# A step table for each group of heads, and norm stages cut into single tiles

## The reference, cut to what matters

```python
x = L0_attn_x
x = x + layernorm(attn(layernorm(x)))        # k, q = latent part + rope part; softmax(q k / sqrt(32)) v; W_O
x = x + layernorm(ffn(layernorm(x)))

def attn(x):
    c_kv, c_q = x @ W_DKV + b_DKV, x @ W_DQ + b_DQ               # latent 128
    k_c, v_c, q_c = c_kv @ W_UK + b_UK, c_kv @ W_UV + b_UV, c_q @ W_UQ + b_UQ
    k_r, q_r = (x @ W_KR + b_KR) * pe, (x @ W_QR + b_QR) * pe    # one rope part for all heads
    ...
    return ctx @ W_O + b_O

def ffn(x):
    # routed: per token the 2 best experts, relu(x @ w_up)^2 @ w_down, weighted
    # shared: relu(x @ shared_up)^2 @ shared_down, with 1024 inner columns
    return routed + shared
```

## Time and profile before

| | |
|---|---|
| Runs | 1718.91, 1721.18, 1721.28 us, median 1721.18 |
| The profiled execution's own time | 1716.51 us |
| Its span (first to last instruction) | 1714.7 us |
| Granted TensorE clock, mean over the span | 0.965 of full |
| Instructions | 22207 |
| DMA | 270.57 MB, mean 158 GB/s |

### The profile page before, as it was taken

How to read it: one execution, slowest core, us unless ns; L and a number is a source line. 1 busy time by engine, 2 the same in 40 slices (tenths; PEclk the granted TensorE clock), 3 DMA queues, 4 the chain that set the end, 5 groups by cost and what they waited for, 6 DMA issues and landing times.

```text
span 1714.7 us, 22207 instructions
## 1 busy us (share of the span) xinstructions
PE 1594.9 (93%) x7386; PEld 1077.0 (63%) x7386; DVE 926.6 (54%) x1896; ACT 836.7 (49%) x1496; POOL 796.5 (46%) x820
## 2 busy tenths in 40 slices
PE   4798999999999899899999789998999999989997
PEld 3454655656556465565654568887666666657886
DVE  3666667575766666766653436445111111128998
ACT  2355456565565565645645434430333333346554
POOL 1167586676766776758669220002222222123341
PEclk9799999999999999999999889997999999989999
DMA  4647367465474663745761252123833433367773
GB/s 120 199 123 200 99 173 225 120 183 156 138 224 124 186 200 99 213 125 166 212 195 73 85 183 87 43 99 96 309 130 128 132 127 129 117 235 255 239 235 129
DMA packets 123767, 270.57 MB, mean 158 GB/s; under 512 B 15396, under 2 KB 27044, under 8 KB 117508
## 3 DMA queue, kind: packets, MB, share of 16 engines
q1 hardware_dynamic: 97256, 205.97, 39.9%
q0 software_dynamic: 12912, 41.82, 7.7%
q10 hardware_dynamic: 13488, 21.37, 3.4%
HBM read 154.03 MB, written 92.01 MB: 143 GB/s over the span
## 4 chain that ended last, share of the span: by engine, by line
PE 67%; DMA 9%; DVE 7%; POOL 7%; issue 5%; SPq 3%; ACT 2%; POOLq 0%; DVEq 0%; ACTq 0%
PE bank L109 10%; PE bank L677 10%; PE bank L733 8%; PE bank L756 8%; PE bank L655 8%; PE bank L592 4%; DMA a<-in_L_attn_x 4%; PE bank L576 4%; PE bank L562 4%; PE bank L581 3%; POOL a L1549 3%; PE bank L716 2%; SPq L1711 2%; DMA a<-kq_scratch 2%; DMA kq_scratch<-a 1%
## 5 line engine op out<-in xcount | busy, mean ns | idle before, releaser
L1549 POOL TENSOR_TENSOR a<-a 128x512 f32<-128x512 f32 x384 | 493.5, 1313 | 83.5 <-ACT a L1352 82.3
L1352 ACT ACTIVATE a<-bank 128x512 f32<-128x512 f32 x512 | 297.4, 597 | 204.0 <-PE bank L581 193.7
L866 DVE TENSOR_REDUCE a<-bank 128x1 f32<-128x512 f32 x512 | 324.0, 680 | 122.3 <-PE bank L562 121.6
L109 PE MATMUL bank<-a 128*128 128x512 f32 (+1 forms) x864 | 238.9, 401 | 8.7 <-DVE a L812 4.0
L576 PE MATMUL bank<-a 128*128 128x512 f32 x512 | 224.7, 439 | 12.3 <-ACT a L1352 12.2
L562 PE MATMUL bank<-a 128*128 128x512 f32 x512 | 188.2, 426 | 29.5 <-DVE a L866 15.1
L581 PE MATMUL bank<-a 68*128 68x512 f32 x512 | 208.2, 407 | 0.2 <-ACT a L1342 0.2
L655 PE MATMUL bank<-c 128*128 128x512 f32 x768 | 186.8, 403 | 21.4 <-ACT c L1404 12.0
L109 PEld LDWEIGHTS bank<-a 128*128 128x128 f32 (+1 forms) x864 | 159.7, 188 | 53.0 <-DVE a L875 4.5
L1621 POOL DMA_INDIRECT f<-h_scratch,f x79 | 75.0, 950 | 251.8 <-PE bank L716 229.1
L655 PEld LDWEIGHTS bank<-c 128*128 128x128 f32 x768 | 148.4, 194 | 59.1 <-issue 12.5
(11 more groups left out here) (186 smaller groups left out, 1896.0 us busy)
## 6 DMA issues: line engine op xcount, KB each, us to landing
a<-kq_scratch SPq DMA_DIRECT2D x192, 256.0 KB, 5.8
kq_scratch<-a SPq DMA_DIRECT2D x32, 1024.0 KB, 4.1
a<-a SPq DMA_DIRECT2D x80, 256.0 KB, 5.3
yp_scratch<-f ACTq DMA_DIRECT2D x79, 256.0 KB, 2.0
a<-in_L_attn_x SPq DMA_DIRECT2D x15, 1024.0 KB, 9.2
x_scratch<-a SPq DMA_DIRECT2D x8, 1024.0 KB, 4.8
h_scratch<-a SPq DMA_DIRECT2D x8, 1024.0 KB, 12.8
hT_scratch<-s SPq DMA_DIRECT2D x8, 1024.0 KB, 8.9
```

What stands on the lines that cost most here:

```text
L109: t = e.matmul(out, a[n], b[n], start=n == 0 and m == 0, stop=n == len(ah) - 1 and m == 2)
L866: e.tensor_reduce(K.mx[:, i, j:j + 1], K.MX[n % 3][:], AX.X, ALU.max).then_inc(Z.max, 1)
L1352: e.activation(K.pt[:, n % NP, :], K.SC[n % 2][:], ACT.Exp, scale=SCALE).then_inc(Z.exp, 1)
L1549: e.tensor_tensor(K.acc[:, j, :], a, K.pt[:, n % NP, :], ALU.add).then_inc(Z.acc, 1)
```

## The change: what it does

`STEP` gets a row of entries for each group (the digit in the name), and the entries count half steps: 2s stands between the scores of step s and its tops, 2s+1 behind the tops; an entry above 31 falls into the next unit. `beside_order` now returns all stages of a unit with their keys, and `attention_order` sorts them. `norm_order` has a stage for each tile: four "stat", one "aggr", "root", four "scale", and for "y" four "residual". The instructions, their sizes and their semaphores are the same. Since `after_order` uses `norm_order`, the list `rest` beside the shared FFN grows from 20 entries to 34.

```diff
@@ -118,7 +118,8 @@
 
 
 def norm_order(kind, b):
-    return [("stat", kind, b, 0), ("stat", kind, b, 1), ("root", kind, b), ("scale", kind, b, 0), ("scale", kind, b, 1)]
+    return ([("stat", kind, b, i) for i in range(4)] + [("aggr", kind, b), ("root", kind, b)]
+            + [("scale", kind, b, i) for i in range(4)] + [("residual", b, i) for i in range(4) if kind == "y"])
 
 
 def half_order(u):
@@ -138,46 +139,79 @@
     return ([("turn", b, k) for k in range(4)], [("proj", b, w) for w in ("kv", "q", "r")], [("v", b, i) for i in range(4)])
 
 
-STEP = {"last values": 2, "total": 2, "invert": 1, "k": 0, "q": 4, "divide": 3, "round": 5, "low": 6, "qr": 0,
-        "turn": (6, 7, 9, 12), "proj": (6, 14), "r": 4, "v": (4, 6, 10, 12), "project": (9, 10, 13, 15), "turn2": (2, 3, 8, 8),
-        "route": 12, "fold": 15, "rows": 14, "n": (0, 1, 3, 6, 9), "y": (0, 3, 4, 6, 7), "h": (0, 0, 2, 4, 7),
-        "values": (7, 11, 14), "tops": (3, 3, 4, 5, 5, 6, 8, 10, 12, 13, 14, 14, 16, 16, 16, 16)}
-
-
-def norm_at(kind, b):
-    return list(zip(STEP[kind], norm_order(kind, b)))
+STEP = {"last values0": 9, "total0": 8, "invert0": 10, "divide0": 2, "round0": 14, "low0": 15, "k0": 1, "q0": 3, "rows0": 27,
+        "values0": (15, 15, 29), "tops0": (3, 4, 5, 6, 6, 7, 10, 11, 14, 14, 16, 16, 16, 16, 16, 16), "last values1": 7,
+        "total1": 7, "invert1": 7, "divide1": 8, "round1": 24, "low1": 18, "k1": 9, "q1": 11, "rows1": 30,
+        "values1": (16, 23, 30), "tops1": (3, 3, 5, 5, 7, 8, 10, 10, 13, 14, 15, 15, 16, 16, 16, 16), "last values2": 7,
+        "total2": 6, "invert2": 8, "divide2": 5, "round2": 17, "low2": 21, "k2": 4, "q2": 5, "rows2": 30,
+        "values2": (12, 21, 31), "tops2": (3, 3, 6, 6, 6, 7, 8, 10, 12, 13, 13, 13, 16, 16, 16, 16), "last values3": 6,
+        "total3": 7, "invert3": 5, "divide3": 12, "round3": 23, "low3": 30, "k3": 0, "q3": 2, "rows3": 28,
+        "values3": (12, 26, 26), "tops3": (3, 4, 4, 4, 4, 5, 7, 9, 11, 13, 14, 15, 16, 16, 16, 16), "turn0": (14, 18, 25, 33),
+        "proj1": (14, 27), "r2": 9, "v3": (11, 13, 21, 22), "turn23": (0, 2, 11, 18), "route3": 26, "fold3": 28,
+        "project0": (19, 24, 29, 35), "qr0": 26, "qr3": 18, "n3": (3, 8, 9, 9, 12, 13, 21, 23, 24, 28),
+        "h2": (0, 0, 0, 1, 1, 0, 8, 11, 14, 20), "y1": (0, 0, 0, 4, 4, 6, 8, 11, 11, 14, 9, 14, 15, 20)}
 
 
 def beside_order(u):
     b, g = u // NG, u % NG
-    at = [(STEP["values"][i], ("values", u, i)) for i in range(3)]
+    at = []
+
+    def put(name, items):
+        where = STEP[f"{name}{g}"]
+        at.extend(((32 * u + n, 1), x) for n, x in zip(where if isinstance(where, tuple) else [where] * len(items), items))
+
+    if g == 0 and b:
+        at.append(((32 * u, -1), ("again", b - 1)))
+    if u == NU - 3:
+        at.append(((32 * u, -1), ("early su",)))
+    if u == NU - 2:
+        at.append(((32 * u, -1), ("early hT",)))
+    for step in range(16):
+        at.append(((32 * u + 2 * step, 0), ("scores", u) + divmod(step, 4)))
+    if u + 1 < NU:
+        due = STEP[f"tops{g}"]
+        for n in range(16):
+            at.append(((32 * u + 2 * next(step for step in range(16) if due[step] > n), 2), ("top", u + 1) + divmod(n, 4)))
+        put("rows", [("rows", u + 1)])
+    put("values", [("values", u, i) for i in range(3)])
     if g >= 3 and b + 1 < B:
-        at += [(STEP["qr"], ("qr", b + 1, 0))]
+        put("qr", [("qr", b + 1, 0)])
     if g == 0 and b:
-        at += [(STEP["qr"], ("qr", b, 1))]
+        put("qr", [("qr", b, 1)])
     if u:
-        at += [(STEP["last values"], ("values", u - 1, 3)), (STEP["last values"], ("keep", u - 1))]
-        at += [(STEP[x], (x, u - 1)) for x in ("total", "invert", "divide", "round", "low")]
+        put("last values", [("values", u - 1, 3), ("keep", u - 1)])
+        for x in ("total", "invert", "divide", "round", "low"):
+            put(x, [(x, u - 1)])
     if u + 2 < NU:
-        at += [(STEP["k"], ("half", u + 2, "k")), (STEP["q"], ("half", u + 2, "q")), (STEP["q"], ("send", u + 2))]
-    if u + 1 < NU:
-        at += [(STEP["rows"], ("rows", u + 1))]
-    if b + 1 < B:
-        at += [[(STEP["turn"][k], ("turn", b + 1, k)) for k in range(4)],
-               [(STEP["proj"][n], ("proj", b + 1, w)) for n, w in enumerate(("kv", "q"))],
-               [(STEP["r"], ("proj", b + 1, "r"))], [(STEP["v"][i], ("v", b + 1, i)) for i in range(4)]][g]
-    if g == 2 and b + 2 < B:
-        at += [(STEP["r"], ("load", b + 2))]
-    if g == 3 and b + 2 < B:
-        at += norm_at("n", b + 2)
-    if b:
-        at += [(STEP["project"][i] - 16 * g, ("project", b - 1, i)) for i in range(4) if STEP["project"][i] // 16 == g]
-        at += [[], norm_at("y", b - 1), norm_at("h", b - 1), [(STEP["turn2"][k], ("turn2", b - 1, k)) for k in range(4)]
-               + [(STEP["route"], ("route", b - 1)), (STEP["fold"], ("fold", b - 1))]][g]
-    found = {}
-    for step, x in at:
-        found.setdefault(step, []).append(x)
-    return found
+        put("k", [("half", u + 2, "k")])
+        put("q", [("half", u + 2, "q"), ("send", u + 2)])
+    if g == 0:
+        if b + 1 < B:
+            put("turn", [("turn", b + 1, k) for k in range(4)])
+        if b:
+            put("project", [("project", b - 1, i) for i in range(4)])
+    elif g == 1:
+        if b + 1 < B:
+            put("proj", [("proj", b + 1, w) for w in ("kv", "q")])
+        if b:
+            put("y", norm_order("y", b - 1))
+    elif g == 2:
+        if b + 1 < B:
+            put("r", [("proj", b + 1, "r")])
+        if b + 2 < B:
+            put("r", [("load", b + 2)])
+        if b:
+            put("h", norm_order("h", b - 1))
+    else:
+        if b + 1 < B:
+            put("v", [("v", b + 1, i) for i in range(4)])
+        if b + 2 < B:
+            put("n", norm_order("n", b + 2))
+        if b:
+            put("turn2", [("turn2", b - 1, k) for k in range(4)])
+            put("route", [("route", b - 1)])
+            put("fold", [("fold", b - 1)])
+    return at
 
 
 def attention_order():
@@ -185,19 +219,7 @@
     out = norm_order("n", 0) + [("sel",), ("split w", "d")] + turns + projs + [("qr", 0, 0), ("qr", 0, 1), ("split w", "u")] + half_order(0)
     out += [("load", 1)] + vs + half_order(1) + [("bias",), ("split w", "o")]
     out += [("top", 0, j, i) for j in range(4) for i in range(4)] + [("rows", 0)] + norm_order("n", 1)
-    for u in range(NU):
-        b, g = u // NG, u % NG
-        if g == 0 and b:
-            out.append(("again", b - 1))
-        if u == NU - 3:
-            out.append(("early su",))
-        if u == NU - 2:
-            out.append(("early hT",))
-        beside = beside_order(u)
-        tops = [("top", u + 1, j, i) for j in range(4) for i in range(4)] if u + 1 < NU else []
-        for step in range(16):
-            out.append(("scores", u) + divmod(step, 4))
-            out += tops[STEP["tops"][step - 1] if step else 0:STEP["tops"][step]] + beside.get(step, [])
+    out += [x for _, x in sorted(sum((beside_order(u) for u in range(NU)), []), key=lambda y: y[0])]
     return out + [("values", NU - 1, 3), ("keep", NU - 1), ("again", B - 1)]
 
 
@@ -779,27 +802,26 @@
     def end(*label):
         return Z.free[K.fill[label] % 2], 1
 
-    def stat(kind, b, half):
-        stats, mv = K.stats[kind], K.mv[kind]
+    def stat(kind, b, i):
+        if kind == "n" and b == 0:
+            w.wait_ge(Z.x0[i], 16)
+        elif kind == "n":
+            w.wait_ge(Z.x, 16 * b)
+        elif kind == "y":
+            n = K.fill["project", b, i]
+            w.wait_ge(Z.free[n % 2], n // 2 + 1)
+        else:
+            w.wait_ge(Z.x1, 4 * b + i + 1)
         src = {"n": K.xt, "y": K.yb, "h": K.xb}[kind]
-        at = {}
-        for i in (2 * half, 2 * half + 1):
-            if kind == "n" and b == 0:
-                w.wait_ge(Z.x0[i], 16)
-            elif kind == "n":
-                w.wait_ge(Z.x, 16 * b)
-            elif kind == "y":
-                n = K.fill["project", b, i]
-                w.wait_ge(Z.free[n % 2], n // 2 + 1)
-            else:
-                w.wait_ge(Z.x1, 4 * b + i + 1)
-            e.bn_stats(stats[:, i, :], src[:, i, :]).then_inc(*small.next())
-            at[i] = small.n
-        if b and not half:
+        e.bn_stats(K.stats[kind][:, i, :], src[:, i, :]).then_inc(*small.next())
+        taken[kind, b, i] = small.n
+
+    def aggr(kind, b):
+        if b:
             w.wait_ge(Z.off[kind], 2 * b)
-        for i in (2 * half, 2 * half + 1):
-            w.wait_ge(Z.small, at[i])
-            e.bn_aggr(mv[:, i, :], stats[:, i, :]).then_inc(Z.var[kind], 1)
+        for i in range(4):
+            w.wait_ge(Z.small, taken[kind, b, i])
+            e.bn_aggr(K.mv[kind][:, i, :], K.stats[kind][:, i, :]).then_inc(Z.var[kind], 1)
 
     def sel():
         w.wait_ge(Z.w2, 7 * 16)
@@ -1286,14 +1308,13 @@
             filled("bias")
         e.copy(high, given).then_inc(Z.w_hi, 1)
 
-    def scale(kind, b, half):
```

(38 more changed lines are left out.)

## The result

The change made the kernel slightly slower: 1726.11 us (median of 7 runs, 1724.68 to 1730.16) against 1718.91 us for the kernel before on the same chip (7 runs, 1715.34 to 1721.28), a ratio of 1.0044, interval 1.0031 to 1.0057. The forecast was 1678. The profiled execution has a span of 1724.8 us, 10.1 more than before.

The account below looks back on a forecast made before the run. PE, busy 93% of 1714.7 us, was taken as the bound, leaving only its waits and slow clock to win. Middle batches 30, batch 0 3, batch 7 4, FFN 10, less 4: 43 off 1721.2, so 1678; range 1660 to 1710.

Parts of the forecast that it names:

- the term for g0 and g1: Pair g0+g1 in each middle batch: from 58.9 us to 56.4, a gain of 2.5 a batch.
- g1's exp waits and slow stretch: In g1, PE's 1.5 us of exp waits and some 1.4 us of slow matmuls behind them should go.
- g0 costs nothing: In g0, POOL's division waits before any sum, but 1.7 us of cover keeps PE from waiting; cost 0.
- Rival C: POOL's late division in g0 makes PE stand and pushes sums into g1; slower, 1741 us; chance 0.08.
- g2: In g2, PE's 2.3 us wait for a DVE reduction goes; unit at 22 to 23.5 us.
- g3's head gives part back: At g3's first top PE waits 1.5 to 2 us for the stack's DMA; g2+g3 falls from 53.4 to 50.7.
- The FFN's first stage: Shared FFN's first stage, 79.1 us: less PE idling and slow clock gains 10 us, bounds 3 and 15; near 69.
- Choosing operations pushed back cost 0: DVE's 28 choosing operations, 9 us, delay the pairs' start to about 1151; 10 us of cover, cost 0.
- The clock rule: Idle gaps bring PE's half clock; if each new g3 wait did, 1.4 us x 7 = 10 more, 1688.
- Sum: Whole kernel: 30 + 3 + 4 + 10 = 47, less 4, gives 43 us gained: 1678.
- Batches 0 and 7: Gains outside the six middle batches: 3 us in batch 0 and 4 in batch 7.
- The 4 us held back: Taken off the summed gain of 47 us for waits not found, since every unit's order is new.

Follow-up runs that it names:

- e10: The changed kernel with one wait added: in g1 POOL's fourth residual waits until `low` is done, all places unchanged; 1662.11 us (4 runs), ratio 0.9665 to before.
- e2: The changed kernel with ACT's rounding in g1 (`round1`) moved from place 24 to 17, ahead of `low1` at 18; 1698.61 us, one run.
- e7: The changed kernel with `low1` moved from place 18 to 62 and `low3` moved to 38; 1661.17 us (4 runs), ratio 0.9656 to before.

## Why the prediction was wrong

**The step that failed** is the term for g0 and g1, "I take 56.4". It takes the exp waits and the slow stretch away, and they did go. But it puts nothing in for DVE behind the aggregates: I walked PE, ACT and POOL through the new g1 and DVE only that far. The pair measured 64.5 us. Two things were missed there:

1. `low1` at 18 lies before `round1` at 24. It is in the diff. By itself it costs 3.37 us of DVE and, in this table, no PE time (e10: pair 55.8).
2. A competition between DVE and POOL for `low`, which I did not weigh at all. The profile before had its trace: `low` has a mean of 1030 ns where a free one takes 0.68 us. The earlier trace rows has another: the rope's subtraction takes 1.57 us on half the partitions, and 0.69 at its shortest, and I took the 1.57 for its own length. All my durations for DVE were of rows where POOL let it in soon. In the new g1, POOL's sums and residuals run without a gap to the unit's end. It costs 7.35 us of PE in g1 and, with the slow stretch behind it, 36.20 - 27.52 = 8.7 us a batch, and 24.09 - 23.22 = 0.9 in g2 (e10's means): 9.5 x 6 = 57, and with the last batch's g1 (35.6 against 28.0) 65, which is the difference of the two spans (1724.8 and 1659.4).

**Everything else, by the steps.** Measured in after where the stall does not reach, else in e10, which has after's order.

- *g1's exp waits and slow stretch*: gone; e10 27.5 us, forecast 27 to 28. The root is out 9.8 us into the unit (10.3), and ACT's first scaling waits 0.25 us for it, not 0.86. Right.
- *g0 costs nothing*: 28.30 us, all of it PE, forecast 29. Rival C, POOL's late division in g0, did not come. Right.
- *g2*: 23.2 in e10, forecast 22 to 23.5; the 2.3 us wait is gone. Right. In after 24.1, the stall's aftermath.
- *g3's head gives part back*: the wait for the stack stays, and in batch 5 there is no bank wait. g2+g3 is 304.70/6 = 50.8 us, forecast 50.7, but here two errors cancel: 0.9 of it is the stall's aftermath, and e10 has 23.22 + 26.75 = 50.0. The mechanism was right and the wait too long in the sum: batch 5's is 1.13 us, not 1.5 to 2. PE's timeline of after, batch 5, then of e10, batch 3, which has the longest of e10's:

```profile
719.21 0.96 PE L584 MATMUL bank<-a 128*128 128x512 f32 x3 [1.13 <-DMA a<-kq_scratch]
```

```profile
457.86 1.10 PE L584 MATMUL bank<-a 128*128 128x512 f32 x3 [2.62 <-DMA a<-kq_scratch]
```

- *The FFN's first stage*: 68.1 us, forecast 69. PE's timeline has `up`'s 32 matmuls in 7.47 us (10.11 before) and, behind the 5.03 us at the start, one long wait left, for h's root:

```profile
986.27 7.47 PE L677 MATMUL bank<-c 128*128 128x512 f32 x32
994.14 6.96 PE L677 MATMUL bank<-c 128*128 128x512 f32 x28 [0.40 <-DVE c L945]
1004.47 4.58 PE L677 MATMUL bank<-c 128*128 128x512 f32 x12 [3.37 <-ACT c L1431]
```

- *Choosing operations pushed back cost 0*: right. The chain that ended last has the pair matmuls without a gap in them (22.40 us before):

```profile
1170.09 22.41 PE bank L727 x128
```

- *The clock rule*: I had asked whether g3's new waits each bring a slow stretch. Behind the 1.13 us wait above, none (clock 1.00), nor behind the 2.04 and 2.13 us ones of after's batches 3 and 4. Behind e10's 2.62 us there is one, in the same view as the earlier trace rows:

```profile
453.40:482.70 29.30, 26.68 (x146) 17.33 (x143) 16.22 (x31) 18.61 (x33) 18.86 (x22) 0.94 0.86 248
```

  It is one unit of six, 1.4 us of busy time more than batch 5's 25.24, so the price was rightly left out of the sum. The rule as the prediction read it from the Trainium skill, "TensorE: Matmul & The Clock Gate", HAM oscillation, that an idle gap brings the half clock, agrees with this one and with the 7.35 us wait of g1, not with the 1.13, 2.04 and 2.13 us ones.
- *Sum*: with the stall taken out, the order gives 1662 us, 16 below the forecast. The six batches gave 39 us where I had 30: g0+g1 3.1 a batch, not 2.5, and g2+g3 3.4, not 2.5. Batches 0 and 7 gave 7 together, as forecast. The 4 us held back were not needed, the FFN stage gave 11 where I had 10, and the median of before was 2 us lower here.

**The chances.** Slower had 0.08, and all of it on POOL in g0. The right mechanism had no rival. It would have been found by asking of each moved stage which instructions of the other engines now run beside it, not only which it waits for.

**What stays open.** Why `low` gets in at once in one batch and is shut out for 12 us in another, with starts that agree to 20 ns against POOL's boundary (e2); why e7's gets in at the second boundary and after's at none of six. The runs show how long a loss can last, to the train's end, not when it must. Whether `low` would be let in by some other gap in the train shorter than e10's 0.69 us was not tried.

## What to carry to other kernels

When an engine's busy time grows and its instruction count doesn't, compare the mean duration of each group between the two profiles before looking at any wait: a competition for a port looks like work, not like idle time. When a stage on DVE with SBUF inputs is moved, look at what POOL does beside it; a train of POOL operations without a gap can hold it off to the train's end, and one wait that makes POOL pause, or another place, was enough here. Two orders that differ in one entry lay 3.7% apart, so a table of places is to be measured by parts.

## What the runs showed of the hardware that I had not expected

- A DVE subtraction of 0.68 us took 8.60 and 12.09 us beside POOL operations of 1.28 us each: it got in at none of six, and none of nine, boundaries between them. The section of the Trainium skill named above says, of operations in a two-port mode, that whoever issues first gets the pair for the whole instruction. It does not say who gets it next. A reader may take it that the one that waits does, which would bound the delay by one sum, 1.3 us; the measurement decides, and here one instruction does not bound it, for the multiplication (8.33 us) any more than for the subtraction.
- A loss need not be long: in e7 the same subtraction lost to one sum and got in at the next boundary (1.83 us).
- When DVE wins, POOL pays once: three sums in 4.24 us, not 3.77.
- A multiplication with one SBUF input is held off like the subtraction with two (8.33 us), a reduction of the same bytes is not (0.69 us).
